# A graph layer's kernel on one core: x laid out a second time by the host, turned, and no transposes in the node stage and the projections

## The reference

```python
xn = layernorm(x)                                  # (x - mean) / sqrt(var + 1e-5)
h = einsum('nd,hdf->nhf', xn, W)                   # 4 heads of 64
a_src, a_dst = (h * att_src).sum(-1), (h * att_dst).sum(-1)
e = leaky_relu(a_src[src] + a_dst[dst], 0.2)       # 206,250 edges, sorted by dst, + loops
alpha = softmax of e over the edges with one dst
gnn = segment_sum(h[src] * alpha, dst) + bias
q, k, v = split(rmsnorm(xn, g_pre) @ w_qkv)        # 3 x 128
mix = rmsnorm(linear_attention(q, k, v) @ w_out + b_out, g_out) + xn
x = x + gnn + mix
x = x + experts(layernorm(x))                      # 8 experts, the 2 best of a node
```

## Time and profile before

| | |
|---|---|
| median of 3 runs | 2605.71 us (2603.78 to 2613.53) |
| span of the profiled execution | 2600.8 us; the profile gives no other time of it |
| GpSimd busy | 1853.9 us, 71% of the span |
| VectorE, TensorE busy | 1559.2 us and 1557.1 us, 60% each |
| ScalarE busy | 693.4 us, 27% |
| first product of the node stage | starts at 18.61 us |
| first gather of the edge stage | starts at 89.18 us |
| first and last product of the projections | 141.4 and 415.6 us |
| last gather | starts at 2290.5 us |
| granted TensorE clock, mean | 0.675 of 2.4 GHz |

### The profile page before, as it was taken

The page is one execution under the profiler, slowest core; times in us unless marked ns, Lnnn a source line. Parts: engine busy times, 40 slices in busy tenths (PEclk is TensorE's granted clock), DMA queues, the critical chain, the costliest instruction groups (busy, mean ns, idle before and its releaser), DMA issues. The chain is left out here.

```text
span 2600.8 us, 54069 instructions
## 1 busy us (share of the span) xinstructions
PE 1557.1 (60%) x17407; PEld 1202.7 (46%) x17407; DVE 1559.2 (60%) x5736; ACT 693.4 (27%) x2061; POOL 1853.9 (71%) x1870
## 2 busy tenths in 40 slices
PE   6666666556666535425434764765666475648893
PEld 4444444535444324323323653544555354537782
DVE  7677776667777655545545665565666656544333
ACT  6422221112222132022113323324322433322220
POOL 2476667777777777777777777777777777755673
PEclk9777786655556555555555866766777677778997
DMA  7355556734555454454455666466666666557886
GB/s 212 99 150 158 154 157 167 208 106 129 164 153 155 139 161 108 108 161 110 109 146 166 176 181 202 140 183 177 178 179 201 182 182 189 163 171 206 241 231 197
DMA packets 286477, 429.03 MB, mean 165 GB/s; under 512 B 72790, under 2 KB 214312, under 8 KB 286060
## 3 DMA queue, kind: packets, MB, share of 16 engines
q0 software_dynamic: 94320, 246.50, 34.8%
q1 hardware_dynamic: 182748, 170.53, 21.7%
q10 hardware_dynamic: 9120, 8.48, 1.0%
HBM read 348.54 MB, written 72.13 MB: 162 GB/s over the span
## 5 line engine op out<-in xcount | busy, mean ns | idle before, releaser
L1088 POOL DMA_INDIRECT region<-node_table,src_idx x1612 | 1574.7, 977 | 588.3 <-issue 467.3
L1291 PE MATMUL ps_p<-region 128*32 128x65 f32 x12896 | 391.3, 289 | 455.1 <-DVE region L1555 454.1
L1291 PEld LDWEIGHTS ps_p<-region 128*32 128x32 f32 x12896 | 302.8, 151 | 555.0 <-DVE region L1555 548.8
L1162 ACT ACTIVATE ps_p<-region 128x16 f32<-128x16 f32 x403 | 75.4, 187 | 1289.8 <-DVE region L1549 1289.3
L1273 PE MATMUL ps_s<-ident,region 128*128 128x128 f32 x403 | 166.6, 414 | 418.1 <-DVE region L1549 411.0
L1563 DVE SCALAR_TENSOR_TENSOR acc<-ps_p,region,acc 128x65 f32 x806 | 192.8, 280 | 291.1 <-issue 285.5
L1555 DVE TENSOR_TENSOR region<-region,ps_p 128x512 f32<-128x512 f32 x403 | 273.4, 678 | 51.9 <-ACT ps_p L1162 50.9
L1273 PEld LDWEIGHTS ps_s<-ident,region 128*128 128x128 f32 x403 | 87.3, 217 | 449.1 <-DVE region L1549 441.7
L1277 PEld LDWEIGHTS ps_s<-region 128*128 128x128 f32 x806 | 195.8, 274 | 58.6 <-issue 32.5
L1547 DVE TENSOR_TENSOR region<-region,ps_s 128x16 f32<-128x16 f32 x403 | 67.9, 169 | 235.4 <-DMA region<-node_table,src_idx 205.5
L1158 ACT ACTIVATE region<-ps_s 128x128 f32<-128x128 f32 x403 | 111.0, 276 | 288.8 <-PE ps_s L1273 287.4
(11 more groups left out here) (347 smaller groups left out, 2634.4 us busy)
## 6 DMA issues: line engine op xcount, KB each, us to landing
region<-in_W_dram SPq DMA_DIRECT2D x84, 512.0 KB, 5.7
region<-node_table,src_idx POOLq DMA_INDIRECT x1612
acc<-in_W_dram SPq DMA_DIRECT2D x28, 512.0 KB
region<-expert_in SPq DMA_DIRECT2D x47, 258.0 KB, 5.9
acc<-base_rows SPq DMA_DIRECT2D x13, 896.0 KB, 6.2
qkv_rows<-region SPq DMA_DIRECT2D x49, 194.0 KB
y_rows<-acc SPq DMA_DIRECT2D x28, 256.0 KB
node_table<-region SPq DMA_DIRECT2D x49, 132.0 KB, 1.7
```

Source lines behind the costliest of these rows:

```text
L1088: pool.indirect_dma_start(out=rows[:, s, j, :], out_offset=None, in_=table[:, :], in_offset=bass.IndirectOffsetOnAxis(ap=src_idx[:, n * SU ...
L1291: m = pe.matmul(ps_p[s % 2][h * WIN:(h + 1) * WIN, 0:HC], wts[:, s % 2, j, h, :], rows[:, s, j, h * HC:(h + 1) * HC], start=j == 0, stop=j ...
```

## The change

The host hands over x twice: in rows, and turned as `xT`, laid out as 128 partitions x 2 halves x 6,272 nodes, so that a tile of it can be a product's operand as it lies.

- **Mean and scale.** (x - mean) W is x times W with its column means taken out. VectorE subtracts the column means once from `w_h` (and from `w_q`, after its scaling by `g_pre`), from column sums that TensorE makes with a matrix of ones (`column_sums`, `centre`). The row's scale is a factor of the result: `rstd` in the node stage's evictions, `r_scale` in the projections'.
- **Node stage.** `unit_rows`, `across` and `rows_back` are gone. TensorE multiplies `xT_group` with `w_h` into four PSUM buffers in turn in place of two. SyncE loads `xT` by groups of 7 tiles (3 buffers, in what the accumulator uses later; 917,504 bytes a group); three of these loads stand among the first loads of x, four between the table's writes. `dst_raw` moves behind `src_idx`. VectorE takes the statistics of whole groups, two groups ahead. The three buffers are cleared after their last use, two by GpSimd, one by ScalarE (1,792 columns each); GpSimd's clearing at the start shrinks from 7,800 columns to 2,424.
- **Projections.** TensorE multiplies tiles of `xT` directly. SyncE loads each again (128 KB), three tiles ahead, in the same queue as the two writes. ScalarE makes x + xn in one operation with its scale 1 + rstd, and evicts q, k and v (384 columns) from PSUM. VectorE is left with the bias and the maximum.

```diff
+            def xT_load(i):
+                if i >= XN:
+                    sp.wait_ge(h_ps, XG * (i - XN + 1))
+                sp.dma_start(xT_group[:, i % XN], g["xT"][:, :, i * XG * P:(i + 1) * XG * P]).then_inc(xT_in[i % XN], 16)
...
             x_load(0)
-            sp.dma_start(dst_raw, g["dst"]).then_inc(dst_in, 16)
+            xT_load(0)
...
             for i in range(1, X_GROUPS):
                 x_load(i)
+                if i < XN:
+                    xT_load(i)
             sp.dma_start(src_idx[:, 0:BLOCKS * SUB], g["src"]).then_inc(src_in, 16)
+            sp.dma_start(dst_raw, g["dst"]).then_inc(dst_in, 16)
 
             for n in range(TILES):
+                if n % XG == 0 and XN <= n // XG + 2 < X_GROUPS:
+                    xT_load(n // XG + 2)
                 sp.wait_ge(h_ready, n + 1)
...
+            for a in range(XT):
+                xT_tile(a)
...
                 sp.dma_start(qkv_rows[a * P:(a + 1) * P, :], qkv[:, a % 2, :]).then_inc(qkv_out[a % 2], 16)
+                if a + XT < TILES:
+                    xT_tile(a + XT)
...
# scalar: node stage
-            for n in range(TILES + 2):
-                if n < TILES:
...
-                    unit_rows(n, xr_ready)
-                if n >= 2:
-                    table_rows(n - 2)
+            for n in range(TILES):
+                if n % XG == XG - 2 and n // XG + 1 < X_GROUPS:
+                    deviation(n // XG + 1)
+                if n % XG == 0:
+                    act.wait_ge(scales, n // XG + 1)
+                table_rows(n)
...
# scalar: projections
-                    act.wait_ge(a_xT_ps, a + 1)
+                    act.wait_ge(a_qkv_ps, a + 1)
                     if a >= 2:
-                        act.wait_ge(a_qkv_ps, a - 1)
-                    act.activation(xrT[:, a % 2, :], ps_x[a % 2][:, 0:DIM], ACT.Copy).then_inc(a_xT, 1)
+                        act.wait_ge(qkv_out[a % 2], 16 * (a // 2))
+                        act.wait_ge(k_seen, a - 1)
+                    act.activation(qkv[:, a % 2, 0:3 * HID], ps_x[2 + a % 2][:, 0:3 * HID], ACT.Copy,
+                                   scale=r_scale[:, a:a + 1]).then_inc(a_qkv, 1)
...
# tensor: node stage
+            pe.wait_ge(weights, 1)
+            column_sums(ps_p[0][:, 0:DIM + 8], w_h)
+            pe.wait_ge(weights, 2)
+            for n in range(TILES):
+                i, j = n // XG, n % XG
+                if j == 0:
+                    pe.wait_ge(xT_in[i % XN], 16 * (i // XN + 1))
+                if n >= 4:
+                    pe.wait_ge(h_ready, n - 3)
                 for c in range(KC):
-                    m = pe.matmul(ps_x[2 + n % 2][:, 0:DIM + 8], xrT[:, n % 2, c * P:(c + 1) * P], w_h[:, c, :],
+                    m = pe.matmul(ps_x[n % 4][:, 0:DIM + 8], xT_group[:, i % XN, c, j * P:(j + 1) * P], w_h[:, c, :],
                                   start=c == 0, stop=c == KC - 1)
...
# vector
+            def centre(w, sums):
+                for c in range(KC):
+                    own.step(dve.scalar_tensor_tensor(out=w[:, c, :], in0=sums, scalar=-1.0 / DIM, in1=w[:, c, :],
+                                                      op0=ALU.mult, op1=ALU.add))
+                own.wait()
...
-                    own.do(dve.scalar_tensor_tensor(out=x_all[:, a, :], in0=xr[:, a % XR, :], scalar=un_scale[:, a:a + 1],
-                                                    in1=x_all[:, a, :], op0=ALU.mult, op1=ALU.add))
-                    dve.tensor_tensor(x_all[:, a, :], x_all[:, a, :], bias_row[:, :], ALU.add).then_inc(a_base, 1)
+                    dve.tensor_tensor(x_all[:, a, :], xr[:, a % XR, :], bias_row[:, :], ALU.add).then_inc(a_base, 1)
...
-                    own.do(dve.tensor_copy(qkv[:, a % 2, 0:3 * HID], ps_x[2 + a % 2][:, 0:3 * HID]))
-                    dve.sem_inc(a_qkv, 1)
+                    dve.wait_ge(a_qkv, a + 1)
```

More of the change, by code:

```diff
@@ L700, in main_stage @@
     XR = 4
+    XT, XN = 3, 3
     A0 = 4
@@ L767, in main_stage @@
     xr = carve(XR, DIM)
[L768 removed]
+    xT_tiles = carve(XT, KC, P)
     w_q = carve(KC, 3 * HID)
@@ L880, in main_stage @@
         self_done = sem("self_done")
-        xr_ready, xT_ps, xT_ready, h_ps, h_ready = sem("xr_ready"), sem("xT_ps"), sem("xT_ready"), sem("h_ps"), sem("h_ready")
+        h_ps, h_ready, w_mean, k_seen = sem("h_ps"), sem("h_ready"), sem("w_mean"), sem("k_seen")
+        xT_in = [sem(f"xT_in{i}") for i in range(XT)]
+        XT_BEFORE = [len(range(i, X_GROUPS, XN)) if i < XN else 0 for i in range(XT)]
         table_out, sd_ready = [sem(f"table_out{i}") for i in range(2)], sem("sd_ready")
@@ L1115, in deviation @@
                 act.activation(s2[:, r], mv[:, r, 1], ACT.Sqrt, scale=float(DIM)).then_inc(sqrts, 1)
-            def unit_rows(n, ready):
-                act.activation(xr[:, n % XR, :], x_all[:, n, :], ACT.Identity,
-                               bias=r_bias[:, n:n + 1], scale=r_scale[:, n:n + 1]).then_inc(ready, 1)
             def table_rows(n):
@@ L1233, in _, with column_sums @@
             pe.wait_ge(consts, 3)
-            def across(n, ready, done):
+            def column_sums(ps, w):
                 for c in range(KC):
-                    m = pe.transpose(ps_x[n % 2][:, c * P:(c + 1) * P], xr[:, n % XR, c * P:(c + 1) * P], ident[:, :])
-                m.then_inc(done, 1)
-            def products(n):
-                pe.wait_ge(xT_ready, n + 1)
-                if n == 0:
-                    pe.wait_ge(weights, 1)
-                if n >= 2:
-                    pe.wait_ge(h_ready, n - 1)
+                    m = pe.matmul(ps, ones[:, :], w[:, c, :], start=c == 0, stop=c == KC - 1)
+                m.then_inc(w_mean, 1)
+            pe.wait_ge(weights, 1)
[7 more added lines that the diff above has]
+                    pe.wait_ge(h_ready, n - 3)
                 for c in range(KC):
-                    m = pe.matmul(ps_x[2 + n % 2][:, 0:DIM + 8], xrT[:, n % 2, c * P:(c + 1) * P], w_h[:, c, :],
+                    m = pe.matmul(ps_x[n % 4][:, 0:DIM + 8], xT_group[:, i % XN, c, j * P:(j + 1) * P], w_h[:, c, :],
                                   start=c == 0, stop=c == KC - 1)
                 m.then_inc(h_ps, 1)
-            for n in range(TILES + 1):
-                if n < TILES:
-                    pe.wait_ge(xr_ready, n + 1)
-                    if n >= 2:
-                        pe.wait_ge(xT_ready, n - 1)
-                    across(n, xr_ready, xT_ps)
-                if n:
-                    products(n - 1)
             pe.wait_ge(smax_ready, 1)
@@ L1440, in tile_stats, with group_stats @@
                 own.step(dve.bn_stats(st[:, n, :], x_all[:, n, :]))
-            for n in range(XG):
-                tile_stats(n)
-            for k in range(3):
-                moments(0, k)
+            def group_stats(i):
+                for n in range(i * XG, (i + 1) * XG):
+                    tile_stats(n)
+                for k in range(3):
+                    moments(i, k)
+            group_stats(0)
             dve.wait_ge(loads, 16 * N_LOADS)
-            logit_weights(0)
-            for k in range(2):
-                unit_scales(0, k)
-            logit_weights(1)
+            for i in range(2):
+                logit_weights(i)
             dve.sem_inc(weights, 1)
-            def rows_back(n):
-                dve.wait_ge(xT_ps, n + 1)
-                if n >= 2:
-                    dve.wait_ge(h_ps, n - 1)
-                dve.tensor_copy(xrT[:, n % 2, :], ps_x[n % 2][:, 0:DIM]).then_inc(xT_ready, 1)
+            unit_scales(0)
+            dve.wait_ge(w_mean, 1)
+            centre(w_h, ps_p[0][:, 0:DIM + 8])
+            dve.sem_inc(weights, 1)
+            for i in range(1, 3):
+                group_stats(i)
             def node_logit(i):
@@ L1461, in node_logit @@
                 dve.sem_inc(sd_ready, 1)
[L1462 to L1480 removed]
+            for i in range(1, X_GROUPS):
+                unit_scales(i)
+                if i + 2 < X_GROUPS:
+                    group_stats(i + 2)
+                elif i + 2 == X_GROUPS:
                     columns_of_blocks()
+                node_logit(i - 1)
             node_logit(X_GROUPS - 1)
```

112 lines of the change are left out of this document (44 added, 68 removed).

## The result

| | before | changed |
|---|---|---|
| median, first measurement (4 runs each) | 2604.74 us | 2578.75 us, ratio 0.9893 (95%: 0.9866 to 0.9920) |
| median, second measurement (21 and 6 runs) | 2604.78 us | 2576.05 us, ratio 0.9893 (0.9876 to 0.9911) |
| span of the profiled execution | 2600.8 us | 2575.0 us |
| first gather / block 60 / last gather | 89.2 / 419.0 / 2290.5 us | 80.6 / 387.5 / 2262.3 us |

The change gains 26.0 us where 28.5 were forecast; 2577.2 us was predicted. The intervals of the two measurements are about 7 and 5 us to either side. The two parts can be seen in the places that the prediction named.

A forecast was written before the change was run, and what follows sets the result against it. GpSimd's gathers were taken as the bound, held back by a late start and, in the projections, VectorE. Gains of 21.0 + 7.5 = 28.5 us take the 2,600.8 us span to 2,572.3, plus 4.9 around it 2,577.2; range 2,563 to 2,592.

The forecast's parts named there:

- What bounds the projections: Projections, 194 to 419 us: VectorE sets the pace at 5.61 us a block and tile; GpSimd's gathers wait for it.
- the 1.22 us that it loses: Projections: VectorE loses a scaled addition (0.52 us) and a 384-column copy (0.70) a tile, leaving 4.39 us, under the gather's 5.03.
- The projections' 21.0 us: Projections: 33.0 us of gather waits, less 39 x 0.305 of issue, leave 21.1 us; 21.0 taken as gain.
- The loads of the turned x at nothing: Projections: 128 KB more a tile, 0.8 us of 5.03 on the DMA engines, is covered and costs nothing.
- The DMA share: Projections: the DMA engines' share goes from 0.56 to about 0.7 with the tile loads.
- The stall of the node stage: Node stage: three loads ahead of group 0's table rows take 7.6 us; rows out at 47.6 us, TensorE idle eight us.
- The slow restart: Node stage: after the idle time TensorE runs 4.4 to 5 us at half speed, 2.4 us lost.
- The end of the stage: Node stage: last eviction ends at 79.0 us against 86.47, a gain of 7.5; first gather at about 82.
- The rival without a stall: Node stage: group 0's rows leave before TensorE wants its buffer; stage ends at 67.7, total 2,565.9 us; chance 16%.
- the rival in which the node stage gives nothing: Node stage: groups wait for their own 1.87 MB at 240 GB/s; stage ends at 86.5, total 2,584.7 us; chance 17%.
- Projections give nothing: Projections: TensorE, at 1.2 GHz, becomes the bound at 5.6 us; only 7.5 us gained, total 2,598.2; chance 9%.
- The sum: Whole kernel: 21.0 us from the projections plus 7.5 from the node stage, 28.5 us, to 2,577.2 us.

The follow-up runs named there:

- f3: Kernel before with only the change's node stage, projections of before: 2596.71 us, ratio 0.9970 to the kernel before.
- f2: The changed kernel, run once more against the kernel before on the same chip: 2576.05 us, ratio 0.9893.
- f4: f3 plus 46 of the change's tile loads, issued into a buffer that nothing reads: 2606.29 us, ratio 1.0002 to the kernel before.
- g1: Changed kernel plus 18 unread products on TensorE ahead of node tile 18, slower chip: 3002.93 us, ratio 0.9993 to the kernel before.
- e4: Changed kernel, edge lists loaded behind 35 table rows, x's last three groups also behind rows, slower chip: 3001.38 us, ratio 0.9990 to the kernel before.
- g2: The same kernel as e4, run again on the slower chip: 3001.31 us, ratio 0.9986 to the kernel before.
- e3: Changed kernel with the edge lists loaded behind the first 35 table rows, slower chip: 3004.09 us, ratio 0.9998 to the kernel before.
- e2: The kernel of f3 on the slower chip: 2998.63 us, ratio 0.9978 to the kernel before.
- e1: Kernel before with only the change's projections, node stage of before, slower chip: 3012.68 us, ratio 1.0024 to the kernel before.

## Why the prediction was right

- **What bounds the projections.** Right. VectorE's pace was read as the cause of GpSimd's waits; f3 keeps VectorE's work and keeps the 32.8 us of waits, the changed kernel takes the work away and 0.6 are left. Without the two operations VectorE waits for the gathers. One reading was not right: VectorE's instructions don't lie nose to tail. In each block it stands idle for 0.93 us before the accumulation, while it reads the block's column (timeline of the kernel before):

```profile
258.98 0.48 DVE L1563 SCALAR_TENSOR_TENSOR acc<-ps_p,region,acc 128x65 f32 x2 [0.93 <-issue]
```

  The profile shows no wait for another engine there, so the pace is still VectorE's own, and the 1.22 us that it loses come off the 5.61.
- **The projections' 21.0 us.** 20.7 by the medians of f3 and f2, with some 6 us to either side; in the profiles of before and after 23.0 by block 60 (31.5 less the 8.5 of the start). Of these, about 21.5 are the waits and 1.5 gathers that took a little less time.
- **The loads of the turned x at nothing.** TensorE never waited for a tile of them, and no cost shows in the changed kernel. But the reason given was incomplete. It asked only whether DMA had room and the gathers grew; f4 shows a price of 0.17 us a block on VectorE, where VectorE is the bound. It is hidden behind the 0.77 us that VectorE had just been given. The DMA share came out at the forecast 0.70 by luck: 0.56 of a block of 5.65 us is 0.62 of one of 5.07, and with the 0.16 reckoned for the loads that makes 0.78. The loads added about half of the 0.16.
- **The stall of the node stage.** Group 0's rows were forecast out at 47.6 us, and ScalarE went on at 46.80. 7.6 us for three loads at 361 GB/s was right in kind: DMA ran at 373 to 388. TensorE began 2.5 us earlier than assumed (column sums at 15.5, not 18.0), which only made the stall longer.
- **The slow restart.** Forecast, and seen: 12 matmuls in 4 us at a clock of 0.57, then 1.00. The rule of the Trainium skill that was cited for it ("TensorE: Matmul & The Clock Gate", section "Why this matters for your kernels") agrees. Its price stands at 2.4 us in the sum; g1, counted from the stall's end, shows 1.5 to 2.9 us against the seven other profiles.
- **The end of the stage.** 79.0 forecast, 77.97 measured; first gather 82 forecast, 80.65 measured; the node stage alone 7.5 forecast, 8.1 measured.
- **The rival without a stall** was priced at 2,565.9, from an end of the stage at 67.7. e4 and g2 removed the stall, and the stage ended at 73.8 to 75.4; 5.1 us of that are the wait for the moved targets. Whether the rival's 67.7 can be reached is open. The 240 GB/s of the rival in which the node stage gives nothing stood on no row, and transfers at 320 to 388 GB/s from 20 to 60 us speak against it.
- **Projections give nothing**, at 9%, didn't happen on chip A. On chip B it did, by something that no row of chip A shows: the block product's release 5.1 us after its start. The rival's shape was right (TensorE's answer becomes the bound), its reason wasn't.
- **The sum.** 28.5 forecast; 26.0 and 28.7 in the two measurements, with some 7 and 5 us of uncertainty.

## What to carry to other kernels

Read a stage's gain from the wait that ends last in it, and check what else is just below that: here removing 1.2 us of VectorE's work a block gained 0.57, since the gather stands at 5.03, and nothing on a chip where the round through the product's release stands at 6.1. A transfer can cost time with room left on the DMA engines, on an engine that takes no part in it; price it with a load that nobody reads, and look for the instruction that got longer. When an experiment moves a load back, check who uses it first and what stands behind that in the same engine's order: in e3 and g2 a list of the edges that arrived late cost 5 us that had nothing to do with the stall under test.

## What the runs showed of the hardware that was not expected

- **Two chips of one kind differ by 400 us on this kernel.** Of the 392 us between the spans of e2 and f3, 388 lie ahead of the last gather, and the pace there is set by the release of the block product: 32 float32 matmuls of 128 rows by 32 columns, four of them side by side on the four quarters of the array's columns, 65 columns wide. From its start to the gather let go it takes 1.40 us on chip A and 5.10 us on chip B. The lateness belongs to this product and what follows it: in e2 the 49 tiles' products of the node stage, which come before the first block, are signalled 0.01 us after their recorded end, as on chip A. "TensorEngine Tiling (Array Packing)" of the Trainium skill, section "Key Properties", says that different tiles can execute in parallel. The trace of chip A agrees (four start within 0.02 us, the next four 0.1 us later); on chip B the recorded starts are the same, but they don't show when the matmuls ended.
- **The profile shows the same 1.09 us for that product on both chips.** Only the releases ("remote" at VectorE and GpSimd) show that anything is late. In the block of e2 shown above, the signals of the five groups of matmuls from the product to the mask's transpose land within 0.18 us, from 253.49 to 253.67, though their recorded ends lie 2.9 us apart.
- **A read of one value into a register takes VectorE 0.3 to 0.6 us in the median, and longer beside more transfers:** 0.57 and 0.31 us in f3, 0.60 and 0.43 in f4.
- **The granted clock and the transfers.** Between 200 and 400 us it was lower in the kernel with more transfers in four pairs (f3 0.80, f4 0.73; before 0.79 and 0.77, changed 0.76 and 0.75; on chip B e2 0.72, e1 0.64). But between 194 and 250 us it was higher in the changed kernel (0.79 against 0.77 and 0.76), and TensorE's work and pace differ in most pairs. No link is shown.
